# First batches of a fused attention and expert kernel: parts stored before the next x, keys loaded from ScalarE's queue, the second norm's rest on GpSimd

## Chip, cores and metric

The kernel runs on one core of a Trainium2 chip. The metric is the device time of one execution in microseconds (us); shorter is better. Engines are named TensorE (PE, with PEld for its weight loads), VectorE (DVE), ScalarE (ACT), GpSimd (POOL) and SyncE (SP), whose queue issues nearly all DMAs.

## The reference

For x of 16 batches x 512 tokens x 256 channels (float32):

```python
xn = layernorm(x)
Q, K, V = relu(xn @ Wq + bq), relu(xn @ Wk + bk), relu(xn @ Wv + bv)    # 16 heads of 16
scores = Q K^T / 4, keys whose xn row sums to zero and later keys masked
out = softmax(scores) V + xn ; attention = gamma * normalised(out) + beta
logits = xn @ router_w.T + experts_bias ; top 2 of 8 experts
ffn = sum over the two experts of softmaxed weight * (silu(xn w1) * (xn w3)) w2 + one shared expert
result = x + attention + ffn
```

## The kernel before, in words

There are two phases: attention for 16 batches, then the experts. The change touches the start of the attention phase alone.

**Iterations.** Every engine has its own program, written as `for i in range(-3, B + 1)`, and each iteration has 44 units, `for s in range(NU)`. In iteration i four batches are under way: batch i in its column scores, exponentials and weighting (`attend`), batch i + 1 in its row scores and row maxima (`maxima`), batch i + 2 in its projection (`project`), batch i + 3 in its layer norm (`norm`). Iteration -3 only norms batch 0, -2 projects batch 0 and norms batch 1, -1 finds the row maxima of batch 0, projects batch 1 and norms batch 2. Iteration 0 is the first with column scores. Tables of unit numbers (`AT_X`, `AT_K`, `AT_MEAN` and so on) say at which unit an engine does which step of projection and norm; between them TensorE makes one unit of row scores and VectorE its row maximum. Engines wait for one another by semaphores only.

**Norm.** VectorE sums rows (`ln_mean`), centres them (`ln_centre`, L825, sets `a_ready`), ScalarE squares, VectorE sums (`ln_var`); GpSimd makes the root of each row from small tiles (128x4). VectorE takes the reciprocal (`ln_rd`, L847), the quotient (`ln_quotient`, L855) and its high bits (`ln_quotient_bits`, L860, sets `q_ready`). What is left is the correction that makes the quotient exact. For the batches below `EARLY` = 2 VectorE does it (`ln_rest`, L871 to L883), for the others GpSimd in six wide operations (`quotient`, L585 to L594); its last one writes xn and sets `normed`.

**Projection.** TensorE transposes xn (L1217, units `AT_X`), ScalarE and VectorE split it into high and low halves (`x_high`, `x_low`), TensorE makes four tiles of queries and keys (`project_tile`, L1211), ScalarE writes each out (`tile_out`, L676 and L677), and GpSimd and ScalarE split it into three bf16 parts (`second`, L495; `second_part`, L682; `third`, L501, sets `b2_done`). Masks of padded tokens come from row sums of xn (`ln_masks`) and four tiny operations and a transpose (`ln_masks_end`, L897 to L906).

**Through DRAM.** The parts go to DRAM and come back with other partitions. SyncE does it in this order in each iteration's second half of its body: store xn, load the x of batch i + 4 (`load_x`, L316, waits for `a_ready`), store the parts of half 0 (`store_parts`, L356, two DMAs), wait until they have landed, store masks (L383, four), load the augmented queries and keys of half 0 (`load_aug`, L393 and L398, fourteen DMAs), store the parts of half 1, bring the negated maxima of half 0 into q_aug (`load_neg`, L408, eight). The loads of half 1 come first in the next iteration. Row scores (L1245, `s_ps`) need `load_aug`, column scores (L1264, `st_ps`) need `load_neg` too.

**Row scores and maxima.** Units with several heads (at most 256 keys) get the causal mask by a product of the identity with the mask (L1242), and VectorE reduces them (L929). Units with one head (512 or 384 keys) get no such product; VectorE adds the mask and takes the maximum in one custom operation (L926).

Of the kernel before, what the change touches and what calls it, by code (L numbers as in the profile page):

```python
# [92 lines left out]
def attention_phase(nc, t, part_dram, xn_dram, expert_rows, plan):  # L93
# [28 lines left out]
    with ExitStack() as ctx:  # L122
# [138 lines left out]
        EARLY, SMALL, SMALL_PARTS = 2, 28, 24  # L261
# [16 lines left out]
        AT_HIGH = (33, 35, 36, 38, 40, 42)  # L278

# [32 lines left out]
        def _(sp):  # L312
# [73 lines left out]
            def load_aug(b, par, tt):  # L386
# [23 lines left out]
            def body(i, par, tail, attend, maxima, project, norm):  # L410
# [45 lines left out]
        def _(pool):  # L456
# [139 lines left out]
            await_(pool, rows_in, 16 * 5)  # L596

            def body(i, par, tail, attend, maxima, project, norm):
# [11 lines left out]
                if project:  # L610
# [36 lines left out]
        def _(act):  # L647
# [53 lines left out]
            def body(i, par, tail, attend, maxima, project, norm):  # L701
                for s in range(NU):
# [9 lines left out]
                    if s in AT_X and project:  # L712
                        x_high(i + 2, AT_X.index(s))
                    if s in AT_K and project:
                        tile_out(i + 2, AT_K.index(s))
                    if s in AT_SECOND and project:
                        second_part(i + 2, AT_SECOND.index(s))
# [4 lines left out]
                    if s == AT_SQUARE and norm:  # L722
# [12 lines left out]
        def _(dve):  # L735
# [185 lines left out]
            def row_maximum(b, u):  # L921
# [3 lines left out]
                if heads == 1:  # L925
# [194 lines left out]
            def body(i, par, tail, attend, maxima, project, norm):  # L1120
                for s in range(NU):
                    if maxima:
# [8 lines left out]
                    if project:  # L1131
# [3 lines left out]
                        if i > -2 and s in AT_X_LOW:  # L1135
                            x_low(i + 2, AT_X_LOW.index(s))
                        if s in AT_MASKS[:2]:
                            ln_masks(i + 2, AT_MASKS.index(s))
                        if s == AT_MASKS[2]:
                            ln_masks_end(i + 2)  # L1140
                        if s in (AT_V_OUT_FIRST if i == -2 else AT_V_OUT):
                            values_out(i + 2, (AT_V_OUT_FIRST if i == -2 else AT_V_OUT).index(s))
# [29 lines left out]
                    if norm:  # L1172
                        if s in AT_MEAN:
                            ln_mean(i + 3, AT_MEAN.index(s))
                        if s == AT_CENTRE:
                            ln_centre(i + 3)
                        if s in AT_VAR:
                            ln_var(i + 3, AT_VAR.index(s))
                        if s == AT_R0:
                            ln_r0(i + 3)  # L1180
                        if s == AT_R1:
                            ln_r1(i + 3)
                        if s == AT_RD:
# [3 lines left out]
                        if s == AT_BITS:  # L1187
# [9 lines left out]
        def _(pe):  # L1197
# [36 lines left out]
            def row_scores(b, par, u):  # L1234
# [6 lines left out]
                if heads > 1:  # L1241
                    mm(v[:, :, keys - P:keys], identb[:], cmask[:, 0:1].to_broadcast([P, heads, P]), start=True,  # L1242
                       stop=False, skip_group_check=True)
                for n in range(heads):
                    last = mm(v[:, n], q_aug[par][0:ROWS_S, h0 + n, P * q:P * (q + 1)],  # L1245
                              k_aug[par][0:ROWS_S, h0 + n, 0:keys], start=heads == 1, stop=n == heads - 1,
# [53 lines left out]
            def body(i, par, tail, attend, maxima, project, norm):  # L1300
                for s in range(NU):

                    b = i + 2
                    if s == AT_ROWS[3] and tail:
# [4 lines left out]
                        output_rows(i - 1, 3)  # L1309
                    if project:  # L1310
                        if s == AT_X[0]:
# [8 lines left out]
                        if s == AT_X[1]:  # L1320
# [742 lines left out]
```

## Time and profile before

| | us |
|---|---|
| median of 3 runs | 1895.26 (1890.43 to 1896.06) |
| the profiled execution | 1895.93 |
| its span | 1894.2 |
| TensorE busy | 1724.7 (91%) |
| VectorE busy | 1274.0 (67%) |
| ScalarE busy | 1090.4 (58%) |
| GpSimd busy | 1173.4 (62%) |

The page gives busy times per engine, and the span in 40 slices of 47 us with the busy share in tenths. A timeline row gives start, duration, engine, line, operation, output<-inputs, and in brackets how long the engine sat idle before it and what released it. A DMA row on SPq shows the time that its issuing took, not the transfer.

### The profile page before, as it was taken

Reading aid. Unit: us, or ns where it says so; the run is one execution under the profiler, and the core shown is the slowest. Engines: PE = TensorE matmul, PEld = TensorE weight load, DVE = VectorE, ACT = ScalarE, POOL = GpSimd, SP = SyncE. Lnnn points to the kernel's source line nnn. Section 1 sums busy time; section 2 is a strip of 40 time slices with the busy share of each in tenths; the row PEclk is TensorE's granted clock in tenths of the full one; section 3 lists DMA queues with packets and bytes.
Section 4 is the critical chain, followed back from the end, with each engine's and each line's share of the span. In section 5 each row is a group of like instructions: output and inputs, shape, how many; then the busy total and the mean of one; then the engine's idle time right before and its main releaser. Section 6 shows DMA issues by size and latency. Waiting matters only on the chain.

```text
span 1894.2 us, 35895 instructions
## 1 busy us (share of the span) xinstructions
PE 1724.7 (91%) x12070; PEld 1293.7 (68%) x12070; DVE 1274.0 (67%) x3089; ACT 1090.4 (58%) x2066; POOL 1173.4 (62%) x1435
## 2 busy tenths in 40 slices
PE   3589999989999999987699999999999998999998
PEld 2345555555555555544388888888888888788887
DVE  6788898888888888867175544544544544466666
ACT  5247666666676666645456666666666675233332
POOL 3465557777777677723467777677677684544443
PEclk9689999999999999988799999999999999999999
DMA  1544344554555445444366667657667664454443
GB/s 53 151 124 136 109 147 147 169 169 138 157 162 166 137 143 166 150 158 160 129 198 209 206 193 233 194 193 232 193 195 231 193 227 145 135 156 145 149 155 99
DMA packets 244224, 310.30 MB, mean 164 GB/s; under 512 B 31466, under 2 KB 209268, under 8 KB 237940
## 3 DMA queue, kind: packets, MB, share of 16 engines
q1 hardware_dynamic: 231796, 274.98, 45.6%
q0 software_dynamic: 12288, 33.57, 5.5%
q8 instruction: 74, 1.21, 0.3%
q14 instruction: 66, 0.54, 0.1%
HBM read 209.60 MB, written 98.34 MB: 163 GB/s over the span
## 4 chain that ended last, share of the span: by engine, by line
PE 43%; ACT 3%; DVE 2%; DMA 1%; POOL 1%; another core or an unknown queue 1%; issue 0%; SPq 0%; DVEq 0%; ACTq 0%
PE gu L1960 27%; PE yp L1974 14%; PE xt L1949 2%; DVE hf L1820 1%; ACT hid_h L1727 1%; DVE passed L1864 1%; ACT sil L1725 0%; ACT w_up_h L1719 0%; DMA w_raw<-in_L_ffn_w_dram 0%; DVE hid_l L1823 0%; DMA w_raw<-in_L_ffn_sw_dram 0%; DVE xc L1831 0%; ACT junk L1784 0%; ACT xc L1733 0%
## 5 line engine op out<-in xcount | busy, mean ns | idle before, releaser
L656 ACT ACTIVATE pT<-st_ps 128x512 f32<-128x512 f32 x682 | 369.0, 562 | 285.1 <-PE st_ps L1266 242.7
L926 DVE CUSTOM_DVE_ANT_0 s_ps<-s_ps,masks 128x384 f32<-128x384 f32 (+1 forms) x512 | 315.0, 632 | 46.8 <-PE s_ps L1245 39.3
L1960 PE MATMUL gu<-xc,w_up_h 128*128 128x512 f32 (+1 forms) x1120 | 339.0, 386 | 6.0 <-DVE hf L1820 4.7
L1820 DVE TENSOR_TENSOR hf<-sil,gu 128x512 f32<-128x512 f32 (+1 forms) x220 | 143.8, 654 | 265.3 <-ACT sil L1725 259.8
L1245 PE MATMUL s_ps<-k_aug,q_aug 97*128 97x512 bf16 (+3 forms) x1024 | 265.5, 312 | 42.8 <-DVE mx L926 15.9
L1264 PE MATMUL st_ps<-q_aug,k_aug 99*128 99x512 bf16 (+1 forms) x992 | 273.3, 308 | 19.0 <-ACT pT L656 10.9
L1823 DVE TENSOR_TENSOR hid_l<-hf,hid_h 128x512 fp32r<-128x512 f32 (+1 forms) x220 | 168.4, 766 | 147.6 <-ACT hid_h L1727 135.7
L1960 PEld LDWEIGHTS gu<-xc,w_up_h 128*128 128x128 f32 x1120 | 205.2, 190 | 51.6 <-issue 6.1
L1727 ACT ACTIVATE hid_h<-hf 128x512 fp32r<-128x512 f32 (+1 forms) x220 | 133.1, 605 | 181.2 <-DVE hf L1820 176.3
L1725 ACT ACTIVATE sil<-gu 128x512 f32<-128x512 f32 (+1 forms) x220 | 123.9, 563 | 194.7 <-PE gu L1960 177.9
L1635 POOL DMA_INDIRECT got<-expert_results,place x128 | 122.8, 959 | 166.1 <-DVE hf L1820 141.3
L1960 PE MATMUL gu<-xc,w_up_l 128*128 128x512 f32 (+1 forms) x560 | 214.2, 382 | 0.0
L1266 PE MATMUL st_ps<-masks,identb 128*128 128x128 bf16 x992 | 196.5, 223 | 0.0
L1960 PE MATMUL gu<-xc,early_high 128*128 128x512 f32 (+1 forms) x640 | 185.5, 375 | 9.6 <-DVE hf L1820 6.2
L488 POOL DMA_INDIRECT expert_rows<-xrow,slot x128 | 127.2, 994 | 97.7 <-ACT pT L656 60.9
L1279 PE MATMUL oT<-pT,v_aug 128*32 128x512 f32 (+3 forms) x2048 | 169.3, 449 | 10.2 <-ACT pT L656 9.7
L1245 PEld LDWEIGHTS s_ps<-k_aug,q_aug 97*128 97x128 bf16 x1024 | 96.5, 100 | 115.3 <-DVE mx L926 34.9
L1627 POOL TENSOR_TENSOR w_up_l<-w_raw,w_up_h 128x512 fp32r<-128x512 f32 x80 | 102.8, 1306 | 94.8 <-ACT w_up_h L1719 82.9
L1974 PE MATMUL yp<-w_dn_h,hid_h 128*128 128x256 f32 x536 | 155.2, 290 | 4.6 <-DVE hid_l L1823 2.9
L1974 PE MATMUL yp<-w_dn_l,hid_h 128*128 128x256 f32 x536 | 152.3, 284 | 0.0
L1974 PE MATMUL yp<-w_dn_h,hid_l 128*128 128x256 f32 x536 | 152.2, 284 | 0.0
L1960 PEld LDWEIGHTS gu<-xc,early_high 128*128 128x128 f32 x640 | 114.5, 190 | 35.6 <-issue 8.6
(259 smaller groups left out, 4041.7 us busy)
## 6 DMA issues: line engine op xcount, KB each, us to landing
early_raw<-in_L_ffn_w_dram SPq DMA_DIRECT2D x60, 512.0 KB
w_raw<-in_L_ffn_w_dram SPq DMA_DIRECT2D x57, 512.0 KB, 5.6
part_scr<-parts SPq DMA_DIRECT2D x64, 384.0 KB
q_aug<-part_scr SPq DMA_DIRECT2D x192, 128.0 KB
k_aug<-part_scr SPq DMA_DIRECT2D x192, 128.0 KB
early_raw<-expert_rows SPq DMA_DIRECT2D x34, 512.0 KB
expert_results<-yo SPq DMA_DIRECT2D x32, 512.0 KB, 3.3
x_sb<-in_L_attn_x_dram SPq DMA_DIRECT2D x16, 512.0 KB, 4.4
```

Source lines behind the costliest of these rows:

```text
L488: gp.indirect_dma_start(expert_rows, bass.IndirectOffsetOnAxis(ap=at, axis=0), xrow[:, b % 2, n], None).then_inc(scattered[b % 2], 16)
L656: fn(pT[j][:, h:h + heads], unit_view(column_bank(b, u), heads, w), ACT.Exp).then_inc(exp_done, 1)
L926: vec.tensor_tensor_reduce(bank[:, 0:keys], bank[:, 0:keys], masks[:, 2 * C + P - keys:2 * C + P], 1.0, LOWEST, ALU.add, ALU.max, mx[:, h ...
L1245: last = mm(v[:, n], q_aug[par][0:ROWS_S, h0 + n, P * q:P * (q + 1)], k_aug[par][0:ROWS_S, h0 + n, 0:keys], start=heads == 1, stop=n == he ...
L1264: mm(v[:, n], k_aug[par][0:ROWS_ST, h, P * j:P * (j + 1)], q_aug[par][0:ROWS_ST, h, P * j:S], start=True, stop=False)
L1266: last = mm(v[:, n, 0:P], identb[:], cmask[:, 1], start=False, stop=True)
L1279: last = mm(oT[32 * n:32 * (n + 1), P * j:S], v_rows[par][:, at:at + 32], pT[j][:, n], start=j == 0, stop=j == NT - 1, tile_position=(0, 3 ...
L1727: fn(hid[par][0][:, m, 0:w], hf[:, m % 2, 0:w], ACT.Copy).then_inc(hh_done, 1)
L1820: vec.tensor_tensor(hf[:, m % 2, 0:w], sil[:, m % 2, 0:w], gu[m % 2][:, 1, 0:w], ALU.mult).then_inc(h_done, 1)
L1823: vec.tensor_tensor(hid[par][1][:, m, 0:w], hf[:, m % 2, 0:w], hid[par][0][:, m, 0:w].bitcast(F32), ALU.subtract).then_inc(hl_done, 1)
L1960: last = mm(gu[m % 2][:, a, 0:width(n)], w_up[wpar][x][:, a, c, P * m:P * (m + 1)], xc[par][:, y, c, 0:width(n)], start=k == 0, stop=k == ...
L1974: last = mm(yp[:, i], hid[par][x][:, m, P * i:P * (i + 1)], w_dn[wpar][y][:, m], start=j == 0, stop=j == 3 * NH - 1)
```

## The change

Five things are changed, all of them for the first iterations:

1. In iteration -2 SyncE stores the masks first, then the parts of half 0; the load of x for batch 2 comes last. GpSimd writes the part of the second tile (`third(i + 2, 1)`) before the small operations of the mean. GpSimd no longer waits at its start for the bias rows.
2. The six loads of batch 0's keys of half 0 are issued from ScalarE's queue, after its fourth part copy (`load_first_keys`).
3. Every row-score unit of batch 0 gets a mask product on TensorE, and VectorE reduces it as it does the others.
4. `EARLY` is 1: the correction of batch 1's norm is done by GpSimd. VectorE's reciprocal, quotient and bits for batch 1 move from the end of iteration -2 to unit 2 of iteration -1.
5. In iteration -1 all steps of projection and norm come `LATE` = 8 units later (`small_unit`).

```diff
-        EARLY, SMALL, SMALL_PARTS = 2, 28, 24
+        EARLY, SMALL, SMALL_PARTS = 1, 28, 24
...
+        LATE, AT_SECOND_QUOTIENT = 8, 2
+
+        def small_unit(i, s):
+
+            return s - LATE if i == -1 else s
...
                     for w, part, dst in ((0, qp, q_aug[par]), (1, kp, k_aug[par])):
+                        if w == 1 and (b, tt) == (0, 0):
+                            continue
...
-                if norm and (not isinstance(i, int) or i + 4 < B):
+                first = i == -2
+                if norm and i + 4 < B and not first:
                     await_(sp, a_ready, i + 4)
                     load_x(i + 4)
+                if first:
+                    store_masks(i + 2)
                 if project:
                     store_parts(i + 2, 0)
                     await_(sp, qk_written[0], 16 * 2 * (i + 3))
+                if project and not first:
                     store_masks(i + 2)
                 if project:
                     if attend:
                         await_(sp, st_scored, NU * i + NU2)
                     load_aug(i + 2, par, 0)
                     store_parts(i + 2, 1)
+                if first:
+                    await_(sp, a_ready, i + 4)
+                    load_x(i + 4)
...
-            await_(pool, rows_in, 16 * 5)
...
                     third(i + 2, 0)
+                if i == -2:
+                    third(i + 2, 1)
                 if norm:
                     small_mean(i + 3)
-                if project:
+                if project and i != -2:
                     third(i + 2, 1)
...
+                        if i == -2 and s == AT_SECOND[3]:
+                            load_first_keys()
...
+            def load_first_keys():
+
+                await_(act, pads, 1)
+                await_(act, qk_written[0], 16 * 2)
+                for n, (_, part) in enumerate(PART_PAIRS):
+                    act.dma_start(k_aug[0][n:ROW_MASK:NPAIR, 0:HH].rearrange("d h n -> d (h n)"),
+                                  part_scr[1, part, 0].rearrange("(d h) n -> d (h n)", h=HT)
+                                  ).then_inc(aug_loaded[0], 16)
...
-                if heads == 1:
+                if heads == 1 and b:
...
-                        if s == AT_CENTRE:
+                        if at == AT_CENTRE:
...
-                        if s == AT_QUOT:
+                        if at == AT_QUOT and i != -2:
                             ln_quotient(i + 3)
...
+                    if i == -1 and s == AT_SECOND_QUOTIENT:
+                        ln_rd(i + 2)
+                        ln_quotient(i + 2)
+                        ln_quotient_bits(i + 2)
...
-                if heads > 1:
+                if heads > 1 or b == 0:
...
-                        if s == AT_X[0]:
+                        if at == AT_X[0]:
                             await_(pe, normed, b + 1)
```

The order of instructions shows three places. On SyncE, in iteration -2, before (x_sb is the next x, part_scr the parts, mask_scr the masks in DRAM):

```order
L316 DMA x_sb<-in_L_attn_x_dram 128x4x256 [waits a_ready]
L356 DMA part_scr<-parts 128x3x512 [waits b2_done] x2
L383 DMA mask_scr<-mkT 8x32 [waits mk_out,qk_written0]
L383 DMA mask_scr<-mkT 8x32 x3
L393 DMA q_aug<-part_scr 16x4096 [waits pads]
L393 DMA k_aug<-part_scr 16x4096
```

And now:

```order
L389 DMA mask_scr<-mkT 8x32 [waits mk_out]
L389 DMA mask_scr<-mkT 8x32 x3
L362 DMA part_scr<-parts 128x3x512 [waits b2_done] x2
L401 DMA q_aug<-part_scr 16x4096 [waits pads,qk_written0]
L401 DMA q_aug<-part_scr 16x4096 x5
L406 DMA q_aug<-mask_scr 1x8x512 [waits mk_stored]
L406 DMA k_aug<-mask_scr 1x8x512
L362 DMA part_scr<-parts 128x3x512 [waits b2_done] x2
L322 DMA x_sb<-in_L_attn_x_dram 128x4x256 [waits a_ready]
```

The masks come first, the loads of k_aug from part_scr are gone from this queue, and the load of x_sb stands behind the stores of half 1.

On VectorE, at the seam of iterations -2 and -1, before (sm holds the small tiles of the norm, s_ps the row scores):

```order
L847 RECIPROCAL sm<-sm 128x4 [waits root_ready]
L848 TENSOR_SCALAR sm<-sm 128x4
L855 TENSOR_SCALAR ln_q<-ln_a,sm 128x256 [waits rd_ready]
L855 TENSOR_SCALAR ln_q<-ln_a,sm 128x256 x3
L860 TENSOR_SCALAR ln_q<-ln_q 128x1024 [waits chain_ln]
L871 SCALAR_TENSOR_TENSOR ln_t<-ln_q,sm,ln_a 128x256 [waits chain_small,q_ready]
L871 SCALAR_TENSOR_TENSOR ln_t<-ln_q,sm,ln_a 128x256 x3
L875 SCALAR_TENSOR_TENSOR ln_t<-ln_q,sm,ln_t 128x256 [waits chain_rest]
L875 SCALAR_TENSOR_TENSOR ln_t<-ln_q,sm,ln_t 128x256 x3
L883 SCALAR_TENSOR_TENSOR xn<-ln_t,sm,ln_q 128x256 [waits xt_ps,mask_part,xn_stored,chain_rest]
L883 SCALAR_TENSOR_TENSOR xn<-ln_t,sm,ln_q 128x256 x3
L926 ISA s_ps,mx<-s_ps,masks 128x512 [waits s_scored]
```

And now:

```order
L957 TENSOR_REDUCE mx<-s_ps 128x1 [waits s_scored] x3
L875 RECIPROCAL sm<-sm 128x4 [waits root_ready]
L876 TENSOR_SCALAR sm<-sm 128x4
L883 TENSOR_SCALAR ln_q<-ln_a,sm 128x256 [waits rd_ready]
L883 TENSOR_SCALAR ln_q<-ln_a,sm 128x256 x3
L888 TENSOR_SCALAR ln_q<-ln_q 128x1024 [waits chain_ln]
L957 TENSOR_REDUCE mx<-s_ps 128x1 [waits s_scored] x12
```

The first three row maxima stand ahead of the reciprocal of batch 1, and the twelve instructions of its correction are gone.

On TensorE, at the start of iteration -1, before (misc<-ident,xn is a transpose of batch 1):

```order
L1245 MATMUL s_ps<-k_aug,q_aug 128x512 [waits aug_loaded0]
L1245 MATMUL s_ps<-k_aug,q_aug 128x512 x2
L1245 MATMUL s_ps<-k_aug,q_aug 128x512 [waits s_max] x2
L1217 MATMUL misc<-ident,xn 128x128 [waits v_out,normed]
L1217 MATMUL misc<-ident,xn 128x128 x3
```

And now:

```order
L1275 MATMUL s_ps<-masks,identb 128x128 [waits s_max]
L1278 MATMUL s_ps<-k_aug,q_aug 128x384
L1275 MATMUL s_ps<-masks,identb 128x128 [waits s_max]
L1278 MATMUL s_ps<-k_aug,q_aug 128x384
L1250 MATMUL misc<-ident,xn 128x128 [waits v_out,normed]
L1250 MATMUL misc<-ident,xn 128x128 x3
L1275 MATMUL s_ps<-masks,identb 128x128 [waits s_max]
L1278 MATMUL s_ps<-k_aug,q_aug 128x384
```

The transposes, with their wait for `normed`, stand behind the thirteenth unit of row scores instead of the fifth, and each unit of one head has a mask product before it.

## Rows read from the trace of the kernel before

**Rows 1.** The page, slices of the whole span, TensorE.
```profile
PE   3589999989999999987699999999999998999998
```

**Rows 2.** Timeline of TensorE: start us, us, line, operation, output<-inputs, [idle before <-releaser].
```profile
64.96 1.46 PE L1245 MATMUL s_ps<-k_aug,q_aug 97*128 97x512 bf16 x3 [12.03 <-DMA k_aug<-mask_scr]
...
112.56 0.56 PE L1264 MATMUL st_ps<-q_aug,k_aug 99*128 99x512 bf16 x1 [2.73 <-DMA q_aug<-negT]
```

**Rows 3.** Timeline of SyncE's DMA queue, first and second batch (start us, us to issue).
```profile
47.10 1.04 SPq L356 DMA_DIRECT2D part_scr<-parts  x2
53.07 1.30 SPq L383 DMA_DIRECT2D mask_scr<-mkT  x4
...
62.74 0.60 SPq L398 DMA_DIRECT2D k_aug<-mask_scr  x1
63.38 0.97 SPq L356 DMA_DIRECT2D part_scr<-parts  x2
67.15 0.54 SPq L393 DMA_DIRECT2D q_aug<-part_scr  x1
...
87.69 0.38 SPq L316 DMA_DIRECT2D x_sb<-in_L_attn_x_dram  x1
...
105.87 5.50 SPq L408 DMA_DIRECT2D q_aug<-negT  x8
```

**Rows 4.** Timeline of VectorE: row sums of batch 0, centring of three, masks of batch 1.
```profile
4.76 1.92 DVE L812 TENSOR_REDUCE lanes<-x_sb 128x32 f32<-128x512 f32 x2 [0.90 <-DMA x_sb<-in_L_attn_x_dram]
...
9.65 1.14 DVE L825 TENSOR_SCALAR ln_a<-x_sb,sm 128x256 f32<-128x256 f32 x4 [1.21 <-POOL sm L525]
...
42.85 3.81 DVE L825 TENSOR_SCALAR ln_a<-x_sb,sm 128x256 f32<-128x256 f32 x4 [4.87 <-POOL sm L525]
...
76.68 1.09 DVE L897 TENSOR_SCALAR msk<-sm 128x4 f32<-128x4 f32 x1 [0.89 <-POOL sm L511]
...
80.03 0.21 DVE L906 STREAM_TRANSPOSE mkT<-mk 128x32 bf16<-128x32 bf16 x1
...
84.87 2.79 DVE L825 TENSOR_SCALAR ln_a<-x_sb,sm 128x256 f32<-128x256 f32 x4
```

**Rows 5.** Timeline of TensorE: the second batch's transposes and projection tiles.
```profile
67.59 1.06 PE L1217 MATMUL misc<-ident,xn 128*128 128x128 f32 x4
...
72.96 1.65 PE L1211 MATMUL misc<-early_high,early_down 128*128 128x512 f32 x6 [1.53 <-DVE early_high L910]
...
80.88 3.01 PE L1211 MATMUL misc<-early_high,early_down 128*128 128x512 f32 x6
```

**Rows 6.** Timeline of VectorE: the second norm's end.
```profile
57.01 0.18 DVE L847 RECIPROCAL sm<-sm 128x4 f32<-128x4 f32 x1 [2.58 <-POOL sm L554]
...
58.45 0.69 DVE L860 TENSOR_SCALAR ln_q<-ln_q 128x1024 uint32<-128x1024 uint32 x1
...
62.59 1.67 DVE L883 SCALAR_TENSOR_TENSOR xn<-ln_t,sm,ln_q 128x256 f32<-128x256 f32 x4
```

**Rows 7.** Timeline of GpSimd: the first mean; parts of the first batch.
```profile
8.00 0.22 POOL L516 TENSOR_TENSOR tree<-lanes 128x16 f32<-128x16 f32 x1 [4.98 <-DMA oTs<-in_L_attn_bk_dram]
...
41.28 0.22 POOL L516 TENSOR_TENSOR tree<-lanes 128x16 f32<-128x16 f32 x1
...
42.77 1.16 POOL L501 TENSOR_TENSOR parts<-early_raw,parts 128x512 bf16<-128x512 f32 x1
43.89 2.37 POOL L495 TENSOR_TENSOR early_raw<-early_raw,parts 128x512 f32<-128x512 f32 x2
```

**Rows 8.** Timeline of ScalarE: the last two part copies of the first batch.
```profile
47.66 1.13 ACT L682 ACTIVATE parts<-early_raw 128x512 bf16<-128x512 f32 x2
```

**Rows 9.** Timeline of VectorE: four reductions of row scores.
```profile
87.58 2.47 DVE L929 TENSOR_REDUCE mx<-s_ps 128x2 f32<-128x512 f32 x4
```

**Rows 10.** Timeline of GpSimd: rest of the third batch's norm, first and last of six.
```profile
102.28 1.89 POOL L585 TENSOR_TENSOR ln_t<-ln_q,sm 128x1024 f32<-128x1024 f32 x1 [1.89 <-issue]
...
113.04 2.34 POOL L594 TENSOR_TENSOR xn<-ln_q,early_raw 128x1024 f32<-128x1024 f32 x1
```

More of the change, by code:

```diff
@@ L711, in body @@
                            ACT.Relu).then_inc(vaug_done, 1)
[L712 to L717, printed above, removed]
+                    at = small_unit(i, s)
+                    if at in AT_X and project:
+                        x_high(i + 2, AT_X.index(at))
+                    if at in AT_K and project:
+                        tile_out(i + 2, AT_K.index(at))
+                    if at in AT_SECOND and project:
+                        second_part(i + 2, AT_SECOND.index(at))
+                        if i == -2 and s == AT_SECOND[3]:
+                            load_first_keys()
                     if s == AT_COPY[0] and attend:
@@ L721, in body @@
                         copy_out(i, 1)
-                    if s == AT_SQUARE and norm:
+                    if at == AT_SQUARE and norm:
                         await_(act, a_ready, i + 4)
@@ L1121, in body @@
                 for s in range(NU):
+                    at = small_unit(i, s)
                     if maxima:
@@ L1134, in body @@
                                 x_low(i + 2, c)
[L1135 to L1139, printed above, removed]
+                        if i > -2 and at in AT_X_LOW:
+                            x_low(i + 2, AT_X_LOW.index(at))
+                        if at in AT_MASKS[:2]:
+                            ln_masks(i + 2, AT_MASKS.index(at))
+                        if at == AT_MASKS[2]:
                             ln_masks_end(i + 2)
-                        if s in (AT_V_OUT_FIRST if i == -2 else AT_V_OUT):
-                            values_out(i + 2, (AT_V_OUT_FIRST if i == -2 else AT_V_OUT).index(s))
+                        if at in (AT_V_OUT_FIRST if i == -2 else AT_V_OUT):
+                            values_out(i + 2, (AT_V_OUT_FIRST if i == -2 else AT_V_OUT).index(at))
                     if group_at(i) is not None:
@@ L1172, in body @@
                     if norm:
-                        if s in AT_MEAN:
-                            ln_mean(i + 3, AT_MEAN.index(s))
-                        if s == AT_CENTRE:
+                        if at in AT_MEAN:
+                            ln_mean(i + 3, AT_MEAN.index(at))
+                        if at == AT_CENTRE:
                             ln_centre(i + 3)
-                        if s in AT_VAR:
-                            ln_var(i + 3, AT_VAR.index(s))
-                        if s == AT_R0:
+                        if at in AT_VAR:
+                            ln_var(i + 3, AT_VAR.index(at))
+                        if at == AT_R0:
                             ln_r0(i + 3)
-                        if s == AT_R1:
+                        if at == AT_R1:
                             ln_r1(i + 3)
-                        if s == AT_RD:
+                        if at == AT_RD and i != -2:
                             ln_rd(i + 3)
-                        if s == AT_QUOT:
+                        if at == AT_QUOT and i != -2:
                             ln_quotient(i + 3)
-                        if s == AT_BITS:
+                        if at == AT_BITS and i != -2:
                             ln_quotient_bits(i + 3)
@@ L1245, in row_scores @@
                     last = mm(v[:, n], q_aug[par][0:ROWS_S, h0 + n, P * q:P * (q + 1)],
-                              k_aug[par][0:ROWS_S, h0 + n, 0:keys], start=heads == 1, stop=n == heads - 1,
+                              k_aug[par][0:ROWS_S, h0 + n, 0:keys], start=heads == 1 and b > 0, stop=n == heads - 1,
                               skip_group_check=True)
@@ L1354, in body @@
                     if project:
-                        if s == AT_V[2]:
+                        if at == AT_V[2]:
                             await_(pe, v_out, NT * b + 2)
                             values(b, 2)
-                        if s == AT_V[3]:
+                        if at == AT_V[3]:
                             await_(pe, v_out, NT * b + 1)
```

15 lines of the change are left out of this document (8 added, 7 removed).

## Prediction

> **What bounds the kernel now.** I read the page first. TensorE is busy 91% of the span, and the slices show where not: the first three (47 us each) hold 3, 5 and 8 tenths, nearly all others 9 [rows 1]. From then on the program is paced by TensorE and what hangs on it, so a change to the first batches can only move the moment at which that steady work begins. The one number to find is the start of iteration 0, its first column scores. The timeline of TensorE has them at 112.56 us, after a wait for q_aug<-negT, the DMAs that bring the negated maxima [rows 2].
>
> Those DMAs stand in SyncE's queue, so I followed that queue backwards [rows 3]. The eight of them go from 105.87 to 111.37. Ahead of them stand the second batch's parts on their way out and back, and ahead of all that the load of the next x (87.69), which waits for VectorE's centring of the third batch, ended at 87.66 [rows 4]. From there to the column scores it is one queue, 24.9 us long. The centring in its turn stands on VectorE behind the second batch's masks, and these behind its normalised rows, xn: TensorE's transposes of xn begin at 67.59 [rows 5]. So the chain is: xn of batch 1, transposes, masks, centring of batch 2, SyncE's queue, column scores: 44.97 us from the transposes on.
>
> Where does 67.59 come from? VectorE ends the rest of the second norm at 62.59 + 1.67 = 64.26 [rows 6]. The first row scores of batch 0 start at 64.96, once their rows are loaded [rows 2], and TensorE has the transposes behind five such units. So xn was ready 3.3 us before it was used. That slack is what the change spends.
>
> **The change, part by part. GpSimd's first wait.** GpSimd began the first mean at 8.00, released by the bias rows, though VectorE's sums were there at 6.7 [rows 4, 7]; without that wait the mean comes 1.3 earlier, and VectorE, which idled 1.21 for it, centres 1.2 earlier. All of the first two norms hangs on that: -1.2. I take it off at the end; the times until then are without it.
>
> **Batch 0's loads.** The parts left at 47.10 although GpSimd had written the second one by 43.93, because the load of x stood ahead. Now it stands behind, and GpSimd writes that part ahead of the small operations that began at 41.28 [rows 7]: 41.3 + 1.16 = 42.5. The stores take 1.04 to issue; then landing took 4.9 us behind an x load (48.14 to 53.07) and 2.8 without one (64.35 to 67.15) [rows 3]. So the parts lie in DRAM at 46.3 to 48.4. SyncE issued fourteen loads from 54.37 to 63.34, 0.64 each [rows 3]; eight are left to it, 5.2 us: 51.5 to 53.6. ScalarE issues the keys' six behind its square and two part copies. The centring ahead of the square now starts at 44.0, beside two GpSimd subtractions that end at 46.3; before, it ended 0.4 behind them [rows 4, 7], so now at 47.0. From the centring to the last copy it took 2.13 us (46.66 to 48.79 [rows 8]): 49.1. Six issues at 0.64 give 52.9. No row shows a DMA issued by ScalarE: the bounds are nothing, below, and twice 0.64 each, above, if the two queues take turns; the 0.64 is nearest, being the same transfer. Last issue to first score took 1.6 (63.34 to 64.96). The first row scores start at about 55, ten microseconds earlier.
>
> By the Trainium skill's page "Perfetto Trace Analysis", section "DMA Instruction — HWDGE", the descriptor generator is locked for one DMA at a time, so two queues would still issue one after the other. By that rule the start would be 57 to 59 instead of 55 (rival B), and no row here shows two queues at once.
>
> **The second norm.** It can't use those ten. Its root was ready at 57.0, now 57.3. VectorE takes the reciprocal and the quotient behind three row maxima (55 + 0.8 + 3 x 0.62 = 57.6, by 2.47 us for four reductions [rows 9]), 2.13 us as before [rows 6]: the quotient is there at 59.8. Then GpSimd does in six wide operations what VectorE did in 5.1 us; the third batch's, from 102.28 to 115.38, took 13.1 [rows 10]. xn of batch 1 is complete at 73.0, not 64.26. TensorE meets its transposes at unit 13 now, not 5. Thirteen units at 0.62, with the quotient's 2.1 between, end near 66, so TensorE waits there some 7 us, and VectorE starves with it. The transposes start at 73.15: **5.55 us later**.
>
> **From there on** the distances stay: each step of projection and norm is 8 units later, and the same number of row maxima stands between masks and centring. Three things change a little. Of the projection tiles one ran in 1.65 us and a later one, after a wait of TensorE, in 3.01 [rows 5]; it now comes out of a long idle stretch: up to 1.35 for each of two tiles. Batch 0's units of one head get a mask product, five on this stretch at 0.1 to 0.2. Against that, tiny mask operations took up to 1.1 us each beside GpSimd's subtractions [rows 4] and may fall clear of them. I take +0.5 for all three. The other 27 mask products, and the eight maxima done early, lie beside SyncE's queue: TensorE already waited 2.73 us for it before the column scores [rows 2], and with eight maxima fewer ahead of them the spare time is 2.73 + 8 x 0.62 = 7.7. That cover gone, the products would cost 27 x 0.2 = 5.4. The load of x for batch 2, now behind the stores, costs nothing: its reader is 20 us away. The quotient of batch 2 shifts with its reader.
>
> **Sum.** 5.55 + 0.5 - 1.2 = 4.85: the column scores start at 117.4, and everything behind them moves along. The profiled execution took 1895.93 us, so 1900.8; the median of the three runs is 1895.26, which gives 1900.1, and I forecast 1900.5. The bounds: below, masks and centring clear of GpSimd (3.56 to 0.85, by 0.17 for each of five operations, and 2.79 to the 1.14 of batch 0 [rows 4]) and a landing of 2.8 instead of 4.9 give back 6.5, so 5.55 - 6.5 - 1.2 = -2.1, 1893.5; above, 2.7 + 1.0 for a slow TensorE, 3.8 for the queues, and nothing from GpSimd's first wait: +13, 1908.5.
>
> **Rivals.** (A) The stretch shrinks. The place is the 20 us from transposes to centring and the landing behind it; if most of those 6.5 us come back, the result is 1893 to 1897. For it: TensorE and VectorE have empty queues when xn arrives. Against it: GpSimd's subtractions still follow the same tiles. 0.15. (B) Slower: the keys' issues share something with SyncE's. Of the fourteen, 9 us, SyncE has done 0.7 to 2.6 when ScalarE begins at 49.1, so they end at 55.3 to 57.3 and the scores start at 57 to 59. It decides from 55 on: every microsecond past that delays quotient, xn and transposes alike, so 2 to 3.8 more, 1902.5 to 1904.5. The lock named above is this case. 0.16. (C) Faster: the ten microseconds are carried through. That needs xn of batch 1 by 63 and the column scores bound by row maxima, not by SyncE's queue: 1895.3 - 10 = 1885. GpSimd's 13.1 us speak against it. 0.06. That the change does not do what it says I exclude: the listed order of instructions shows each move.
>
> **Numbers.** The forecast, column scores 3 to 7 us later, has 0.63. About 0.3% (5.7 us) is what a measurement of this kernel can tell from no change; 0.39 of it lies within, 0.24 above. With B slower is 0.40; with most of A (0.11) same is 0.50; C and the rest of A are 0.10 faster. The range 1891 to 1906 leaves out C and the corner where the upper bounds meet. It is wide below because the fastest of the three runs was 4.8 us under their median.
>
> **What would show it.** Right: first row scores near 54; six wide GpSimd operations from 59 to 72; TensorE idle from 65 to 72 before the transposes; column scores near 117 after a wait for q_aug<-negT. Wrong: no wait for xn, column scores released by something else, or later iterations that make up for a late start.

## The result, and the profile after

| | us |
|---|---|
| median after, 11 runs | 1898.0 (1896.16 to 1900.81) |
| median before, 11 runs | 1893.81 (1890.43 to 1896.06) |
| ratio | 1.0023, 95% interval 1.0015 to 1.003 |
| profiled span after | 1897.5 (before 1894.2) |
| first row scores | 51.65 (before 64.96 [rows 2]) |
| first column scores | 117.29 (before 112.56 [rows 2]) |

The kernel became 0.23% slower, within 0.3%: what was forecast, in sign and size. The page's slices of TensorE start emptier, 2, 5 and 7 tenths for 3, 5 and 8 [rows 1], and are about as full as before from the fourth on:

```profile
PE   2579999999999999987699999999999999999998
```

The timeline of TensorE shows both ends of the story. The row scores now start at 51.65, 13.3 us sooner. The transposes of batch 1 wait 8.69 us for xn from GpSimd and start at 70.33 for 67.59 [rows 5], and the column scores come at 117.29 after a wait for q_aug<-negT, with 6 us of unused time before them:

```profile
51.65 0.23 PE L1275 MATMUL s_ps<-masks,identb 128*128 128x128 bf16 x1 [0.77 <-DMA k_aug<-part_scr]
...
70.33 1.11 PE L1250 MATMUL misc<-ident,xn 128*128 128x128 f32 x4 [8.69 <-POOL xn L609]
...
117.29 0.61 PE L1297 MATMUL st_ps<-q_aug,k_aug 99*128 99x512 bf16 x1 [6.01 <-DMA q_aug<-negT]
```

GpSimd, which began its first mean at 6.77 for 8.00 [rows 7], has the six wide operations where the forecast put them, 13.09 us from the first to the end of the last, as in the third batch [rows 10]:

```profile
6.77 0.22 POOL L531 TENSOR_TENSOR tree<-lanes 128x16 f32<-128x16 f32 x1 [3.76 <-DVE lanes L840]
...
57.19 1.89 POOL L600 TENSOR_TENSOR ln_t<-ln_q,sm 128x1024 f32<-128x1024 f32 x1 [1.33 <-issue]
...
67.94 2.34 POOL L609 TENSOR_TENSOR xn<-ln_q,early_raw 128x1024 f32<-128x1024 f32 x1
```

VectorE's timeline shows what releases them (three maxima, then the reciprocal, waiting for GpSimd's root), and the masks and the centring 24 us later, which answer to [rows 4]. In front of the centring stand two operations that make the negated maxima (L967, L971); before, they stood behind it (the last row is the kernel before's L943, the same operation as L971):

```profile
52.27 1.88 DVE L957 TENSOR_REDUCE mx<-s_ps 128x1 f32<-128x512 f32 x3
54.91 0.18 DVE L875 RECIPROCAL sm<-sm 128x4 f32<-128x4 f32 x1 [0.77 <-POOL sm L569]
...
79.45 1.10 DVE L925 TENSOR_SCALAR msk<-sm 128x4 f32<-128x4 f32 x1 [0.77 <-POOL sm L526]
80.59 1.09 DVE L928 TENSOR_SCALAR mq<-msk 128x4 f32<-128x4 f32 x1
81.59 0.16 DVE L929 TENSOR_SCALAR mk<-msk 128x4 bf16<-128x4 f32 x1
81.67 1.12 DVE L930 TENSOR_SCALAR mk<-msk 128x4 bf16<-128x4 f32 x1
...
87.16 0.19 DVE L967 TENSOR_SCALAR nm<-mx 128x32 bf16<-128x32 f32 x1
...
87.86 1.00 DVE L971 SCALAR_TENSOR_TENSOR nm<-mx,nm 128x32 bf16<-128x32 f32 x1
88.78 3.01 DVE L853 TENSOR_SCALAR ln_a<-x_sb,sm 128x256 f32<-128x256 f32 x4
```

```profile
93.67 0.20 DVE L943 SCALAR_TENSOR_TENSOR nm<-mx,nm 128x32 bf16<-128x32 f32 x1
```

Of SyncE's queue [rows 3] the parts now leave at 39.08, the load of x comes last, and from the next load of x (91.82) to the negated maxima (110.28) it takes 18.46 us, 18.18 before:

```profile
39.08 1.50 SPq L362 DMA_DIRECT2D part_scr<-parts  x2
42.78 4.04 SPq L401 DMA_DIRECT2D q_aug<-part_scr  x6
...
48.24 3.12 SPq L362 DMA_DIRECT2D part_scr<-parts  x2
51.41 0.49 SPq L322 DMA_DIRECT2D x_sb<-in_L_attn_x_dram  x1
...
91.82 0.38 SPq L322 DMA_DIRECT2D x_sb<-in_L_attn_x_dram  x1
...
110.28 5.82 SPq L416 DMA_DIRECT2D q_aug<-negT  x8
```

ScalarE's queue issues the keys meanwhile. Its rows overlap SyncE's of 42.78 to 46.82, and also ScalarE's own activations (44.64 to 46.73):

```profile
44.64 1.06 ACT L743 ACTIVATE ln_t<-ln_a 128x1024 f32<-128x1024 f32 x1 [3.48 <-DVE ln_a L853]
44.70 1.20 ACTq L756 DMA_DIRECT2D k_aug<-part_scr  x2
...
46.12 0.61 ACT L698 ACTIVATE parts<-early_raw 128x512 bf16<-128x512 f32 x1
46.57 1.96 ACTq L756 DMA_DIRECT2D k_aug<-part_scr  x3
```

### The profile page after: what moved, and what is told of

The parts are those of the page before. It is cut to its first block, busy times and chain, and to the rows that moved or that the text cites. A ratio compares the mean times of both kernels' runs of the same rounds, so it can differ in the third digit from the quotient of the medians.

```text
span 1897.5 us, 35921 instructions
## 1 busy us (share of the span) xinstructions
PE 1725.1 (91%) x12102; PEld 1294.4 (68%) x12102; DVE 1268.6 (67%) x3045; ACT 1089.2 (57%) x2066; POOL 1182.0 (62%) x1441
## 4 chain that ended last, share of the span: by engine, by line
PE 43%; ACT 3%; DVE 2%; DMA 1%; another core or an unknown queue 1%; POOL 1%; issue 0%; SPq 0%; DVEq 0%; ACTq 0%
PE gu L1994 27%; PE yp L2008 14%; PE xt L1983 2%; DVE hf L1854 1%; ACT hid_h L1761 1%; DVE passed L1898 1%; ACT sil L1759 0%; ACT w_up_h L1753 0%; DMA w_raw<-in_L_ffn_w_dram 0%; DMA w_raw<-in_L_ffn_sw_dram 0%; ACT junk L1818 0%; DVE hid_l L1857 0%; DVE xc L1865 0%; ACT xc L1767 0%
## 5 line engine op out<-in xcount | busy, mean ns | idle before, releaser
L954 DVE CUSTOM_DVE_ANT_0 s_ps<-s_ps,masks 128x512 f32<-128x512 f32 (+1 forms) x480 | 295.6, 633 | 49.7 <-PE s_ps L1278 37.2
L1278 PE MATMUL s_ps<-k_aug,q_aug 97*128 97x512 bf16 (+3 forms) x1024 | 265.1, 311 | 25.8 <-issue 15.5
L957 DVE TENSOR_REDUCE mx<-s_ps 128x2 f32<-128x512 f32 (+3 forms) x224 | 142.0, 673 | 28.7 <-PE s_ps L1278 28.2
```

Source lines behind the costliest of these rows:

```text
L954: vec.tensor_tensor_reduce(bank[:, 0:keys], bank[:, 0:keys], masks[:, 2 * C + P - keys:2 * C + P], 1.0, LOWEST, ALU.add, ALU.max, mx[:, h ...
L957: vec.tensor_reduce(mx[:, h // HH, q, h % HH:h % HH + heads], unit_view(bank, heads, keys), AX_X, ALU.max).then_inc(s_max, 2)
```

## The experiments

The state to explain: column scores 4.73 us later, total 4.2 us (0.23%) later. The first question was whether GpSimd's 13 us are the cause, or the shift by 8 units that goes with them.

Each trace is of one execution, and single executions scatter. Up to the first row scores nine of the kernels have the same instructions in iteration -2 (the changed one, e1, e2, e4, e5, e6, e8, e9, e12); their row scores start between 51.65 and 53.60. e2 and e12 are one kernel: its column scores came at 108.00 and at 108.41. A difference below about 1 us between two traces says little by itself.

**e1, the second norm's rest back on VectorE, shift kept.**

```diff
-        EARLY, SMALL, SMALL_PARTS = 1, 28, 24
+        EARLY, SMALL, SMALL_PARTS = 2, 28, 24
...
                         ln_quotient_bits(i + 2)
+                        if i + 2 < EARLY:
+                            ln_rest(i + 2)
```

> The changed kernel with EARLY = 2: VectorE does the rest of the second norm again, right behind its quotient in unit 2 of iteration -1; all else as changed, LATE = 8 too. Theory (the start of column scores is the second batch's transposes plus some 47 us of a fixed chain, and GpSimd's 13.1 us set the transposes): xn is complete at 57.05 + 5.1 = 62.2; seven more row maxima (0.6 and 0.5 us) stand before unit 13, so the transposes come at about 66.3 instead of 70.33, column scores at 113.3 instead of 117.29, the time 4.0 us under the changed kernel, ratio to before about 1.000. Rival (the mask products, the shift by 8 units or the queue set the start): column scores stay at 117, ratio 1.0023.

Measured: 1895.5 us, ratio 1.0003 (0.9994 to 1.0013). The transposes, at 67.57, came 1.3 later than expected (the row scores had started at 53.31, 1.7 later than in the changed kernel's trace), the column scores, at 113.26, where they were expected.

**e2, the same without the shift** (`LATE` = 0).

> As e1_rest_vector, and LATE = 0. Theory: TensorE meets the transposes behind five units and waits for xn alone: 62.3; the negated maxima no longer stand ahead of the centring, so the chain from there is 45.0 us again, column scores at 107.3, 5.3 us before those of the kernel before, ratio about 0.997. Rival (the eight maxima done early are needed, because VectorE's maxima then end last): column scores later than 110, released by VectorE or by nothing from SyncE's queue, ratio 0.9985 or more.

Measured: 1890.22 us, ratio 0.9968 (0.9959 to 0.9977). VectorE's rest ends at 62.65, and the transposes follow at once:

```profile
62.71 1.11 PE L1252 MATMUL misc<-ident,xn 128*128 128x128 f32 x4 [7.44 <-DVE xn L911]
...
108.00 0.61 PE L1299 MATMUL st_ps<-q_aug,k_aug 99*128 99x512 bf16 x1 [3.64 <-DMA q_aug<-negT]
```

**e6, the changed kernel with `LATE` = 0**, rest still on GpSimd, fills the fourth field.

> The changed kernel with the work of the iteration before the first no longer moved back by 8 units; the second norm's rest stays on GpSimd. If the shift of 8 is not itself what delays, the transposes stay at 70.3 (GpSimd's 13.1 us set them), the chain behind them takes 45 to 46 us, the column scores start at about 115.6, and the ratio is about 1.0013. If the shift is needed, because work of later units then stands in the engines' orders behind waits for the late rows, the column scores start later than 117.3 and the ratio is above 1.0025.

Measured: 1896.69 us, ratio 1.0011 (1.0002 to 1.002); transposes 71.19, column scores 115.88. (In this execution the parts left at 39.89, 0.8 later than in the changed kernel's, and the transposes follow.) The four fields, column scores and ratio:

| rest on | shift 8 | no shift |
|---|---|---|
| GpSimd | 117.29, 1.0023 | 115.88, 1.0011 |
| VectorE | 113.26, 1.0003 | 108.00, 0.9968 |

The rest on GpSimd costs 4.0 us at the column scores with the shift and 7.9 without; at the transposes it is 2.8 and 8.5. The shift costs 5.3 on top of VectorE's rest. On top of GpSimd's it seems to cost 1.4, but that can't be read from these traces: in e6 the masks fell clear of GpSimd's subtractions, and in the other three fields they did not. They took 0.16 or 0.17 each, and the centring started 15.53 us behind the transposes for 17.07 in e2. e4 below shows such a difference to be worth 1.9 us. The first projection tile of e6 ran at half clock (the tile, then the last mask):

```profile
76.55 2.93 PE L1244 MATMUL misc<-early_high,early_down 128*128 128x512 f32 x6 [0.93 <-DVE early_high L938]
```

```profile
80.85 0.16 DVE L930 TENSOR_SCALAR mk<-msk 128x4 bf16<-128x4 f32 x1
```

The two ratios on GpSimd's line overlap in their intervals too. The shift is no cover for the late xn: the instructions behind a wait come late anyway, and with VectorE's rest the shift adds units in front of it.

**e12, e2 once more, in another session.**

> The fast version once more (second norm's rest on VectorE, no shift by 8), unchanged, in a session of its own, because the kernels of the last session came out about 0.001 slower against the kernel before than their traces' early stretch says. If the ratio belongs to the version, it is 0.9968 again within its interval, 0.996 to 0.998. If sessions differ by as much as the intervals, it lies above 0.998, and no difference below 0.002 between sessions is then to be read.

Measured: 1890.32 us against 1896.18, ratio 0.9973 (0.9965 to 0.9982); column scores 108.41. The gain belongs to the version.

**e3, the kernel before without GpSimd's first wait** (the line `await_(pool, rows_in, 16 * 5)` taken out).

> The kernel before without GpSimd's wait for the bias rows. Theory: all steps of the first two norms come 1.2 us earlier, column scores at 111.3, ratio 0.9994. Rival: the weights' splitting holds VectorE, nothing moves, column scores at 112.5.

Measured: 1894.19 us, ratio 0.999 (0.9979 to 1.0001). The transposes come at 65.60 and the column scores at 110.58, both 2.0 us sooner and not 1.2. Batch 0's norm gains 1.3 at its end, and the projection behind it another 0.5 (its first twelve products took 5.00 us for 5.49).

**e4, batch 0's units of one head masked by VectorE's custom operation again**, without mask products:

```diff
-                if heads == 1 and b:
+                if heads == 1:
...
-                if heads > 1 or b == 0:
+                if heads > 1:
```

> The changed kernel with the custom operation for batch 0's units of one head, no mask products for them. Theory: they lie beside SyncE's queue; column scores within 0.5 us of 117.29, ratio 1.002. Rival: 32 products at 0.1 to 0.2 us are on the path, column scores 3 to 5 us earlier, ratio 1.000.

Measured: 1898.03 us, ratio 1.0012 (1.0002 to 1.0021); column scores 114.71, 2.58 sooner than in the changed kernel and not within 0.5 of it as expected; the total can't be told from the changed kernel's. It isn't the products' own time that counts. Transposes start at 70.33 in both, out of 8 us of idle TensorE. With the products TensorE was busy 1.86 of the 2 us from 73 and was granted 0.99 of full speed, 2.4 GHz, in the next three; without them it was busy 1.53, and the clock stayed at its half level, 1.2 GHz (the last three numbers of a windows row are clock, DMA share and GB/s, the first after the length is TensorE's busy time). The changed kernel first:

```profile
73.00:75.00 2.00, 1.86 (x9) 1.06 (x7) 1.74 (x4) 0.60 (x1) 0.00 (x0) 0.50 0.00 0
75.00:78.00 3.00, 2.33 (x12) 1.76 (x13) 3.00 (x5) 0.57 (x1) 0.00 (x0) 0.99 0.00 0
```

```profile
73.00:75.00 2.00, 1.53 (x8) 0.76 (x5) 2.00 (x6) 0.60 (x1) 0.00 (x0) 0.50 0.05 15
75.00:78.00 3.00, 2.65 (x6) 1.83 (x6) 2.77 (x4) 0.00 (x0) 0.15 (x1) 0.50 0.01 3
```

So the first projection tile took 2.93 us in this execution and 1.67 in the changed kernel's. That the products made the difference is not shown. They are in e8 and e9 too, which have the same instructions here, idle 7.05 us each before the transposes and start them at 63.53 and 63.24; the tile is granted 0.50 in e8 and 1.00 in e9 (e6 above, with products, is another slow one):

```profile
68.88 2.93 PE L1251 MATMUL misc<-early_high,early_down 128*128 128x512 f32 x6 [0.93 <-DVE early_high L943]
```

```profile
68.60 1.64 PE L1251 MATMUL misc<-early_high,early_down 128*128 128x512 f32 x6 [1.38 <-DVE early_high L943]
```

What follows from the slow tile can be read. ScalarE's copy of the tile, for which GpSimd waits, comes later. GpSimd's first subtraction starts at 79.70, not 79.37, and VectorE's masks have slipped ahead of it but for the last (e4's VectorE and GpSimd, then the changed kernel's GpSimd):

```profile
79.42 0.16 DVE L925 TENSOR_SCALAR msk<-sm 128x4 f32<-128x4 f32 x1
...
79.76 1.14 DVE L930 TENSOR_SCALAR mk<-msk 128x4 bf16<-128x4 f32 x1
...
86.93 2.97 DVE L853 TENSOR_SCALAR ln_a<-x_sb,sm 128x256 f32<-128x256 f32 x4
```

```profile
79.70 1.17 POOL L510 TENSOR_TENSOR early_raw<-early_raw,parts 128x512 f32<-128x512 f32 x1 [0.60 <-ACT early_raw L693]
```

```profile
79.37 2.28 POOL L510 TENSOR_TENSOR early_raw<-early_raw,parts 128x512 f32<-128x512 f32 x2
81.61 1.15 POOL L516 TENSOR_TENSOR parts<-early_raw,parts 128x512 bf16<-128x512 f32 x1
...
87.65 1.17 POOL L516 TENSOR_TENSOR parts<-early_raw,parts 128x512 bf16<-128x512 f32 x1
```

In the changed kernel the masks (rows above) end at 80.55, 81.68 and 82.79; GpSimd's operations end at 80.5, 81.65 and 82.76, and the one from 87.65 to 88.82 holds L971 (87.86 to 88.86). Three of the four 128x4 operations, 0.16 us by themselves, last until the GpSimd operation that was there first ends. The Trainium skill's page "SBUF — State Buffer", section "SBUF: two separate sides", calls the port pair that VectorE and GpSimd share an exclusive lock, held for a whole instruction. The ends above agree with that; which VectorE operations take the pair, these rows don't show.

In e4 the masks are done 1.9 us sooner (80.90 for 82.79) and the centring starts 1.85 sooner; the other 0.73 of the 2.58 lies behind the centring. The fourteen traces agree on the pattern: where the first tile took 2.5 to 2.9 us (e4, e6, e8, e10, e11) at least three of the four mask operations took 0.16 or 0.17, and where it took 1.6 to 1.7 (the other nine) three of the four took 1.1.

**e5, the negated maxima behind the centring** in iteration -1.

```diff
-                        if s in AT_NEGATE[0]:
-                            minus_maxima(i + 1, 0, AT_NEGATE[0].index(s))
+                        first_half = (24, 25, 26) if i == -1 else AT_NEGATE[0]
+                        if s in first_half:
+                            minus_maxima(i + 1, 0, first_half.index(s))
```

> The changed kernel, with the negated maxima of the second norm's first half behind the centring in the iteration before the first, instead of ahead of it. If 1.2 us of the longer chain are these two instructions in front of the centring, the centring starts about 1.1 us sooner (87.6 for 88.8), the column scores of iteration 0 at about 116.1 (117.29 in the changed kernel), and the ratio to before is about 1.0017. If the centring waits for its input anyway, or the two instructions only come in another's way later, it starts at 88.5 or after and the column scores stay at 117.3.

Measured: 1897.84 us, ratio 1.0019 (1.001 to 1.0028); centring 87.75, column scores 115.65. The centring came as expected, the column scores 1.64 sooner. In the total it can't be told from the changed kernel.

**e7, the keys from SyncE's queue again.**

```diff
-                        if w == 1 and (b, tt) == (0, 0):
-                            continue
...
-                        if i == -2 and s == AT_SECOND[3]:
-                            load_first_keys()
```

> The changed kernel with batch 0's keys' rows loaded from SyncE's queue again, behind the queries' rows. If ScalarE's queue issues beside SyncE's, this costs about 1.7 us at the first row scores (53.3 for 51.65); the root is ready 0.77 us after the maxima, which absorbs some of it, so the quotient on GpSimd begins about 0.9 later, the transposes at 71.2 and the column scores at about 118.2; ratio about 1.003. If the two queues take turns at the issuing, the row scores start at 51.7 or before and nothing moves.

Measured: 1898.69 us, ratio 1.0021 (1.0012 to 1.0031). Row scores 52.96 (+1.3), transposes 70.72 (+0.4), both less than expected, and the column scores came sooner, 116.28, since the centring took 2.07 us for 3.01 this time and the issue of the eight DMAs 5.50 for 5.82. ScalarE's queue is worth nothing in the total. It ended the issuing of the last load at 48.53 for 51.51, but of these 3.0 us only 1.3 reached the row scores (counted from the store of the parts, the nine traces with two queues have them 12.6 to 13.8 us later and e7 14.1, so 0.3 to 1.5), and SyncE's next two stores took 3.12 us to issue (0.97 in e7). From 48 to 51.6 the DMA engines are busy 0.95 with two queues and 0.61 with one (changed kernel, then e7):

```profile
48.00:51.60 3.60, 2.88 (x12) 2.57 (x12) 0.56 (x3) 0.00 (x0) 3.21 (x8) 0.56 0.95 269
```

```profile
48.00:51.60 3.60, 2.67 (x12) 2.36 (x11) 0.66 (x4) 0.00 (x0) 3.11 (x7) 0.62 0.61 184
```

**e10 and e11, the order alone.** e10 is the kernel before with the first item of the change but GpSimd's first wait kept; e11 drops that wait too.

```diff
+                if first:
+                    store_masks(i + 2)
                 if project:
                     store_parts(i + 2, 0)
...
                     store_parts(i + 2, 1)
+                if first:
+                    await_(sp, a_ready, i + 4)
+                    load_x(i + 4)
```

> The kernel before, with one part of the change alone: for batch 0 the masks and parts are stored ahead of the load of x, and GpSimd takes the second part's subtraction ahead of the small mean. Loads from SyncE's queue alone, custom mask operation, second norm's rest on VectorE at its old place, no shift by 8, GpSimd's first wait kept. If the late x.first order was what held batch 0's row scores, these start near 54.5 (64.96 before), and the transposes at the end of VectorE's rest, 64.3 (67.59 before), the column scores at 109.3 for 112.56, ratio about 0.998. If the early row scores are nothing without the rest of the change, the column scores stay above 111.5 and the ratio at 1.000.

> The same, and GpSimd's first wait for the bias rows taken out. If the two gains add (3.3 and 2.0), the column scores start at about 107.3, as early as with the whole change and the rest on VectorE without the shift (108.0), and the ratio is about 0.9967; then the keys' queue, the mask products and the early maxima are worth nothing here. If they are needed, the column scores come after 109 and the ratio is 0.998 or more.

Measured: e10 1891.89 us, ratio 1.0001 (0.999 to 1.0011; one of its twelve runs took 1974.31 us and is not in the ratio), column scores 110.22; e11 1889.89 us, ratio 0.9995 (0.9984 to 1.0006), column scores 109.11. The row scores of e10 start at 55.43 and then stop, because VectorE's rest stands ahead of its first maximum; the transposes, behind five units, start at 66.22 and not at 64.3:

```profile
55.43 1.46 PE L1254 MATMUL s_ps<-k_aug,q_aug 97*128 97x512 bf16 x3 [2.28 <-DMA k_aug<-mask_scr]
65.17 1.25 PE L1254 MATMUL s_ps<-k_aug,q_aug 97*128 97x512 bf16 x2 [8.28 <-DVE mx L935]
66.22 1.06 PE L1226 MATMUL misc<-ident,xn 128*128 128x128 f32 x4
```

So the early maxima do matter: with three of them ahead of the quotient the transposes follow xn at once (e2). By their column scores the two should gain 2.3 and 3.5 us; the measurement shows none for e10 (at most 1.9) and allows 3.0 for e11. In that session the kernel before ran at 1891.68 us, 2.1 to 4.5 us under its medians elsewhere. e12 excludes that e2's gain was such a matter of session. For e10 and e11 the gap stays open, but the traces offer a reason: both are executions with a slow first tile and masks clear of GpSimd, with 15.29 and 15.43 us from transposes to centring for 17.28 in the kernel before. Without these 2.0 and 1.9 us they would gain 0.35 and 1.6, which the totals would fit. How often the masks fall clear in the executions that were not traced, no run shows.

**e8, e2 with the second load of x put off too**: in iteration -1 the parts and masks are stored first, that load comes behind the negated maxima's, and GpSimd writes the second part ahead of the small mean.

> The fast version (rest on VectorE, no shift by 8), with in the iteration before the first also: the parts stored ahead of the load of x, that load behind the load of the negated maxima, and the small mean of GpSimd behind the sums that the store needs. If SyncE's queue and the landing of its transfers set the column scores of iteration 0, they land about 3.5 us sooner, the row maxima (end near 104.3) bind next, the column scores start at 104.5 (108.0 without it) and the ratio is about 0.995. If the later load of x delays batch 2's norm, the gain is given back in iteration 0 and the ratio stays at 0.997.

Measured: 1888.43 us, ratio 0.9967 (0.9958 to 0.9976). The column scores started at 104.84, as expected, and five units later TensorE waited 3.41 us for the third norm's rest:

```profile
104.84 0.38 PE L1304 MATMUL st_ps<-q_aug,k_aug 99*128 99x512 bf16 x1
...
111.07 1.11 PE L1257 MATMUL misc<-ident,xn 128*128 128x128 f32 x4 [3.41 <-POOL xn L614]
```

The gain of 3.2 us was lost there; the next load of x starts at 131.95, in e2 at 130.85.

**e9, e8 with the third norm's rest on VectorE** (`EARLY` = 3).

> The version with the second load of x put off, and with the third norm's rest on VectorE too. There the third norm's rest on GpSimd (13.1 us, ended 111.0) held the transposes 3.41 us behind the column scores. If that wait is the last of the chain, VectorE's 5.1 us cost less than they free and the ratio falls to 0.995; if VectorE's row maxima bound the column scores, they move from 104.8 to about 109.5 and the ratio stays at 0.997 or rises.

Measured: 1887.04 us, ratio 0.9976 (0.9967 to 0.9986), column scores 109.77: VectorE's row maxima bind now, the second of the two cases. e8's ratio is e2's. e9's is 0.0008 above it, with overlapping intervals and in the session of e10 and e11, so neither is shown to beat e2 or to lose to it.

## Why the prediction was right, point by point

**Size and sign.** Column scores +4.85 forecast, +4.73 seen; and the total 4.2 later. 1900.5 was forecast and 1898.0 measured; 1.45 of that difference is the kernel before, whose median over 11 runs was 1893.81 and not 1895.26. That the column scores came within 0.12 of the forecast is luck: the transposes came 1.61 sooner than forecast and the chain behind them 1.49 longer.

**GpSimd's first wait, -1.2.** Undersized: e3 shows -2.0 in its trace (its ratio, 0.999, allows anything from none to 4 us).

**Batch 0's loads.** Row scores forecast at 54 with the first wait taken off, 51.65 seen. The parts left sooner (39.08 for 41.3), and the keys' issues began at 44.70, beside ScalarE's square and copies, not behind them as I had it.

**The second norm, transposes +4.35 with the first wait, seen +2.74.** The step that failed: I had the quotient wait for three maxima. They ended at 54.15, before the root (54.91), so the root set it. The bits were written by 57.05, where my steps give 58.6; that 1.55 is the difference. The wrong wait is the smaller part of it: with the root as the last wait my numbers give 56.1 (57.3 less 1.2) and bits at 58.2. The other 1.2 is the root itself, which came that much sooner than I had it, 0.8 of it by the first wait's size. The 13.1 us on GpSimd, the idle TensorE behind unit 13 and the wait for xn are as forecast, and e1, e2 and e6 show GpSimd's rest to be the cause.

**The chain to the column scores, +0.5, seen +1.99.** The cold tiles I priced did not come: the tiles took 1.63 to 1.74, where [rows 5] had 1.65 and 3.01; what came instead I had not looked for. I said the same number of row maxima stands before the centring, but not that the shift carries it behind the negated maxima: with their collision, centring starts 18.45 us after the transposes for 17.28 (+1.17), and e5 gives 1.00 of it back. L971 took 1.00 beside GpSimd's operation, and the same operation took 0.20 in the kernel before. The centring itself is +0.22, SyncE's queue +0.28, the issue of its eight DMAs +0.32. The masks did not fall clear of GpSimd.

**Hidden work.** The 27 other mask products and the early maxima lie in the spare time, which was 6.0 us where I had 7.7. e4 confirms the spare time, 6.23 us idle without the products for 6.01. Whether the five on the stretch cost something, it doesn't settle: its centring came 1.85 sooner because of the slow tile, and the products aren't shown to decide that. The late load of x cost nothing.

**The whole shift passes to the end.** In these two executions not quite. Loads of x in SyncE's queue, before and after:

```profile
183.49 0.38 SPq L316 DMA_DIRECT2D x_sb<-in_L_attn_x_dram  x1
...
238.35 0.38 SPq L316 DMA_DIRECT2D x_sb<-in_L_attn_x_dram  x1
```

```profile
188.59 0.38 SPq L322 DMA_DIRECT2D x_sb<-in_L_attn_x_dram  x1
...
241.95 0.38 SPq L322 DMA_DIRECT2D x_sb<-in_L_attn_x_dram  x1
```

They are 5.10 us apart at the first and 3.60 at the second, and the spans differ by 3.3. The iteration between them took 54.86 before and 53.36 after. The windows show where: each time TensorE idles (busy 1.14 of 4 us, and 1.36 of 4), and then works for a while at the half level, 1.2 GHz. That low spell is shorter after:

```profile
216.00:220.00 4.00, 1.14 (x6) 0.69 (x6) 3.32 (x13) 1.02 (x3) 0.00 (x0) 0.81 0.46 138
220.00:226.00 6.00, 6.00 (x31) 2.63 (x31) 5.74 (x16) 1.57 (x3) 0.00 (x0) 0.56 0.26 85
```

```profile
220.00:224.00 4.00, 1.36 (x8) 0.43 (x6) 3.60 (x15) 1.73 (x4) 0.00 (x0) 1.00 0.68 197
224.00:230.00 6.00, 5.74 (x34) 2.78 (x35) 5.80 (x17) 1.57 (x3) 0.00 (x0) 0.72 0.06 8
```

The missing clock is 0.19 x 4 + 0.44 x 6 = 3.4 us before and 0.28 x 6 = 1.7 after; the difference is about the 1.5 us regained. That the clock is the cause is read from these rows; no run tried it. And the shorter spell is not shown to come from the change: for the same iteration e2 took 53.33 us and e12, the same kernel, 54.77, with a granted clock of 0.97 and 0.94 (179.3 to 233). So the 1.5 us may be nothing but scatter between executions.

**Rival A**, the stretch shrinks: it grew by 1.99, and the masks did not fall clear. In e6, e10 and e11 they did, and the stretch was 15.3 to 15.5 us: the mechanism is real, though it gave 2 us there and not 6.5. **Rival B** (the 0.7 to 2.6 us that SyncE had done at 49.1 should be 0.7 to 2.8; the ends hold): SyncE's six loads took 4.04 us, a pitch of 0.67 for 0.64 alone, while ScalarE issued at 0.61 to 0.65. The page's rule, which the prediction took from the Trainium skill's "Perfetto Trace Analysis", section "DMA Instruction — HWDGE", would have them take turns; this trace does not show that (five of SyncE's six took 0.58 to 0.61 and one 0.85). Nor do SyncE's slow stores (48.24 to 51.36), since ScalarE's last issue had ended at 48.53. What was longer with two queues was the landing (3.1 us from the last key issue to the row scores, 1.6 before, 1.45 in e7). **Rival C**, the ten microseconds carried through, fell as reasoned: by the root, then GpSimd. e2 carries 4.6 of them through.

## What to carry to other kernels

When work moves to a slower engine, look first at whether its result is already late; here 13.1 us on GpSimd replaced 5.1 on VectorE on the chain that set the column scores, while the other parts of the change together gain 0.3% once that work stays on VectorE and nothing is shifted. A shift by units moves an instruction past its neighbours in the engine's order as well as in time: list which ones it now stands behind. And a step freed by one change is bounded by the next input that is late, so compare all its inputs, not the one you had in mind. Before reading 2 us out of two traces, look whether two executions of one kernel differ by as much.

## What was not expected of the hardware

- Two queues issue side by side, six DMAs in 4.04 us beside 0.61 each, but the row scores then waited 3.1 us behind the last issue for 1.45 with one queue, and SyncE's next two stores took 3.12 us to issue for 0.97.
- A DMA of ScalarE's queue is issued while ScalarE's own activations run (44.70 beside 44.64 to 45.70).
- Several of VectorE's smallest operations last until GpSimd's running operation ends, 1.1 us for 0.16 (masks) and 1.00 for 0.20 (L971), so 0.3 us of timing elsewhere decided 1.9 us at the centring.
- Behind the same instructions and the same 7.05 us of idle, TensorE's first projection tile ran at 2.4 GHz in one execution (1.64 us, e9) and at 1.2 GHz in another (2.93 us, e8).
